# End of the first layer of a two-layer graph kernel: the last tile's scores and sums put ahead of older pairs' norms and tables, its own rows gathered first, the late diagonals made by VectorE

## What is computed

```python
h = relu(layernorm(x))
Qn = cos_normalize(h @ Wq.T);  Kn = cos_normalize(h @ Wk.T)
att = softmax(where(adj > 0, Kn @ Qn.T, NEG), axis=1)
x = x + 0.5 * (att @ h) + 0.5 * h          # first layer; a row with no edge keeps h
h = relu(layernorm(x))
g = h @ W.T + b_W
e = leaky_relu((g @ a1)[:, None] + (g @ a2)[None, :] + b_a)      # slope 0.2
x = x + softmax(where(adj > 0, e, NEG), axis=1) @ g              # second layer
```

## Time and profile before

| what | value |
|---|---|
| median of 3 runs | 1582.53 us (1582.44 to 1582.91) |
| the profiled execution | 1582.28 us, its span 1580.3 us |
| TensorE busy, share of the span | 1084.1 us, 69% |
| VectorE | 1142.5 us, 72% |
| ScalarE | 964.1 us, 61% |
| GpSimd | 1078.5 us, 68% |
| last piece of the adjacency matrix has landed | 805 us |
| first gather of the second layer | 891.49 us |

### The profile page before, as it was taken

How to read it: one execution, slowest core, us unless ns; L and a number is a source line. 1 busy time by engine, 2 the same in 40 slices (tenths; PEclk the granted TensorE clock), 3 DMA queues, 4 the chain that set the end, 5 groups by cost and what they waited for, 6 DMA issues and landing times.

```text
span 1580.3 us, 21879 instructions
## 1 busy us (share of the span) xinstructions
PE 1084.1 (69%) x5729; PEld 815.3 (52%) x5729; DVE 1142.5 (72%) x4489; ACT 964.1 (61%) x2795; POOL 1078.5 (68%) x1121
## 2 busy tenths in 40 slices
PE   6977777788867877877775456556555665555556
PEld 4653545555555555554565335445444554445445
DVE  6995698879887888888776256566666676656666
ACT  5663867778778777877678644454445444544423
POOL 2246777677776767776676377777777777777774
PEclk9997899989999988999888666787788777777777
DMA  9999999999999999999942122222222222222221
GB/s 361 421 388 390 374 399 400 403 347 400 398 394 365 399 399 377 399 398 402 395 169 53 44 55 61 61 60 61 58 61 60 61 59 60 61 60 60 59 60 41
DMA packets 90474, 358.45 MB, mean 227 GB/s; under 512 B 23653, under 2 KB 36328, under 8 KB 57576
## 3 DMA queue, kind: packets, MB, share of 16 engines
q1 hardware_dynamic: 49128, 277.05, 44.1%
q0 software_dynamic: 34304, 71.42, 17.2%
q10 hardware_dynamic: 6912, 8.52, 1.5%
HBM read 344.18 MB, written 12.72 MB: 226 GB/s over the span
## 4 chain that ended last, share of the span: by engine, by line
POOL 36%; DMA 27%; issue 14%; PE 11%; DVE 6%; ACT 5%; SPq 0%; ACTq 0%; POOLq 0%; DVEq 0%
DMA arena<-in_adj_dram 25%; POOL arena L542 19%; POOL arena L537 13%; PE ps L1029 5%; POOL arena L967 3%; DMA arena<-tab,idx_shared 2%; PE ps L1052 2%; POOL arena L975 2%; ACT prod L1217 2%; PE ps L1064 1%; PE ps L1066 1%; DVE norm L1381 1%; ACT R L1187 1%; ACT R L1185 1%; PE ps L1010 1%
## 5 line engine op out<-in xcount | busy, mean ns | idle before, releaser
L967 POOL DMA_INDIRECT arena<-tab,idx_own x320 | 322.2, 1007 | 128.5 <-issue 92.4
L542 POOL DMA_INDIRECT arena<-tab,idx_own x320 | 303.0, 947 | 97.5 <-issue 97.5
L1029 PE MATMUL ps<-arena,fold 128*128 128x512 fp8e4 x1024 | 285.8, 414 | 108.4 <-DMA arena<-in_adj_dram 108.2
L607 ACT ACTIVATE arena<-arena,negm 128x773 f32<-128x773 f32 (+1 forms) x64 | 58.5, 914 | 362.8 <-DVE negm L681 362.8
L975 POOL DMA_INDIRECT arena<-tab,idx_shared x216 | 210.5, 974 | 93.3 <-issue 57.5
L537 POOL DMA_INDIRECT arena<-tab,idx_shared x216 | 204.1, 945 | 87.4 <-issue 65.5
L557 PE MATMUL ps<-prod,column 128*128 128x384 f32 (+1 forms) x128 | 103.2, 905 | 231.2 <-DVE prod L633 231.2
L1029 PEld LDWEIGHTS ps<-arena,fold 128*128 128x128 bf16 x1024 | 91.7, 101 | 258.7 <-DMA arena<-in_adj_dram 153.5
L1217 ACT ACTIVATE prod<-prod,arena 128x128 f32<-128x128 f32 x528 | 203.4, 390 | 0.0
L633 DVE TENSOR_TENSOR prod<-ident,arena 128x384 f32<-128x384 f32 (+3 forms) x70 | 39.5, 571 | 220.7 <-DMA arena<-tab,idx_shared 220.7
L580 PEld LDWEIGHTS ps<-arena,diag 128*128 128x128 f32 x640 | 142.8, 315 | 45.6 <-issue 40.9
(11 more groups left out here) (202 smaller groups left out, 2496.7 us busy)
## 6 DMA issues: line engine op xcount, KB each, us to landing
arena<-in_adj_dram SPq DMA_DIRECT2D x256, 1024.0 KB
arena<-tab,idx_own POOLq DMA_INDIRECT x640, 2.7
arena<-tab,idx_shared POOLq DMA_INDIRECT x432, 2.6
tab<-arena ACTq DMA_DIRECT2D x16, 260.0 KB, 7.4
tab<-tw ACTq DMA_DIRECT2D x32, 130.0 KB
res<-in_x_dram SPq DMA_DIRECT2D x8, 512.0 KB, 11.8
out_dram<-arena SPq DMA_DIRECT2D x64, 64.0 KB, 1.7
prod<-in_L_gnn_Wq_dram SPq DMA_DIRECT2D x1, 64.0 KB
```

What stands on the lines that cost most here:

```text
L542: pool.indirect_dma_start(out=GO[q][:, s, :], out_offset=None, in_=tab1, in_offset=bass.IndirectOffsetOnAxis(ap=idx_own[:, t, s:s + 1], ax ...
L607: nc.scalar.activation(sc[p][:, 0:K + n * P], sc[p][:, 0:K + n * P], ACT.Exp, bias=negm[:, p:p + 1]).then_inc(s_ex1, 1)
L967: pool.indirect_dma_start(out=G[t % GR][:, s, :], out_offset=None, in_=tab0, in_offset=bass.IndirectOffsetOnAxis(ap=idx_own[:, t, s:s + 1] ...
L1029: last = nc.tensor.matmul(keys_ps[t % 2], fold[:, PIECE_BITS * f + b, :], ring8[m % RING][:, b * WORDS:(b + 1) * WORDS], start=False, stop ...
```

## The change

It touches only the end of the first layer, and one order in `scalar_rows`.

1. **Diagonals.** `diags` of tiles 58 and later leave ScalarE. VectorE makes them as one product of 640 elements a partition, identity times the spread weights, right behind `spill_weights` of the same tile; `last_diags` of tile 63 is two such products (three slots, two slots).
2. **Gathers.** GpSimd gathers tile 63's own slots before its shared chunks.
3. **ScalarE.** Tile 63's own scores come first, then its shared ones, all before the transposed copy of pair 28 and the rows of pair 28.
4. **TensorE.** The sums of tiles 62 and 63 stand directly behind those of tile 61, ahead of the projection of pair 28 and of pair 29. Within tile 63 the own part comes first.
5. **VectorE.** Tile 63's own products come ahead of the spill weights of tile 62, its shared product behind all diagonals, its spill weights ahead of `finish` of tile 61.
6. **`scalar_rows`.** For every pair the store is issued right behind `tw`, and the second column follows.

```diff
+    LATE = T - 6
...
                 nc.scalar.activation(tw[:, :, 0:D + 1], got_ps[:, :, 0:D + 1], ACT.Copy).then_inc(self.rows, 1)
+                act.wait_ge(self.rows, 2 * i + 1)
+                act.dma_start(self.rows_at(tab1, 2 * i, 2), tw[:, :, :]).then_inc(self.stored, 16)
                 nc.scalar.activation(s1_all[:, 2 * i:2 * i + 2], got_ps[:, :, D + 1], ACT.Identity,
                                      bias=c0[:, :]).then_inc(self.rows, 1)
-                act.wait_ge(self.rows, 2 * i + 2)
-                act.dma_start(self.rows_at(tab1, 2 * i, 2), tw[:, :, :]).then_inc(self.stored, 16)
...
                 pool.wait_ge(s_pv, T - GR)
-                gather_shared(T - 1)
                 gather_own(T - 1, 0, 3, s_g[0][(T - 1) % GR])
                 gather_own(T - 1, 3, K, s_last)
+                gather_shared(T - 1)
...
                 def weighted_last(t):
                     p, q, n = t % 2, t % GR, PAIRED[t % QT]
-                    pe.wait_ge(s_W, paired(t + 1))
                     pe.wait_ge(s_fin, t - 1)
-                    for j in range(n):
-                        v, s, e = shared(t, SPAN[t % QT][0] + j)
-                        nc.tensor.matmul(pv_ps[p][:, 0:ROW], W[p][j], Gc[:, e, :], start=j == 0, stop=False)
                     for part, (a, b) in enumerate(((0, 3), (3, K))):
                         pe.wait_ge(s_dg, t + 1 + part)
                         for s in range(a, b):
-                            last = nc.tensor.matmul(pv_ps[p][:, 0:ROW], diag[t % DR][:, s, :], G[q][:, s, :], start=False,
-                                                    stop=s == K - 1)
+                            nc.tensor.matmul(pv_ps[p][:, 0:ROW], diag[t % DR][:, s, :], G[q][:, s, :], start=s == 0,
+                                             stop=False)
+                    pe.wait_ge(s_W, paired(t + 1))
+                    for j in range(n):
+                        v, s, e = shared(t, SPAN[t % QT][0] + j)
+                        last = nc.tensor.matmul(pv_ps[p][:, 0:ROW], W[p][j], Gc[:, e, :], start=False, stop=j == n - 1)
                     last.then_inc(s_pv, 1)
...
                 weighted(T - 3)
+                weighted(T - 2)
+                weighted_last(T - 1)
                 second.tensor_pr(pe, PAIRS - 4)
-                weighted(T - 2)
                 second.tensor_tr(pe, PAIRS - 3)
                 second.tensor_pr(pe, PAIRS - 3)
-                weighted_last(T - 1)
...
-                    if t >= 2:
+                    if 0 <= t - 2 < LATE:
                         diags(t - 2)
...
                 second.scalar_hT(act, PAIRS - 5)
-                weights(T - 2)
+                scores(T - 2, 0, slots(T - 2))
+                exps(T - 2)
                 second.scalar_h(act, PAIRS - 4)
                 second.scalar_rows(act, PAIRS - 5)
-                last_scores(T - 1, K, slots(T - 1), 1)
-                last_exps(T - 1, K, slots(T - 1), 3, 1)
+                last_scores(T - 1, 0, 3, 1)
+                last_exps(T - 1, 0, 3, 3, 1)
+                last_scores(T - 1, 3, K, 2)
+                last_exps(T - 1, 3, K, K, 2)
                 second.scalar_root(act, PAIRS - 3)
+                last_scores(T - 1, K, slots(T - 1), 2 + len(runs(T - 1)))
+                last_exps(T - 1, K, slots(T - 1), slots(T - 1), 3)
                 second.scalar_hT(act, PAIRS - 4)
-                last_scores(T - 1, 0, 3, 2)
-                last_exps(T - 1, 0, 3, 6, 2)
-                last_diags(T - 1, 0, 3, 2)
                 second.scalar_h(act, PAIRS - 3)
                 second.scalar_rows(act, PAIRS - 4)
-                last_scores(T - 1, 3, K, 3)
-                last_exps(T - 1, 3, K, 8, 3)
-                last_diags(T - 1, 3, K, 3)
                 second.scalar_hT(act, PAIRS - 3)
...
+                def diags(t):
+                    if t >= DR:
+                        dve.wait_ge(s_pv, t - DR + 1)
+                    dve.wait_ge(s_ex, t + 1)
+                    nc.vector.tensor_tensor(diag[t % DR][:, 0:K, :], repeat(ident[:, :], K), spread(weight[t % 4][:, 0:K], P),
+                                            ALU.mult).then_inc(s_dg, 1)
...
                     if t >= 3:
                         spill_weights(t - 3)
+                        if t - 3 >= LATE:
+                            diags(t - 3)
...
+                def last_diags(t, first, end, n):
+                    dve.wait_ge(s_ex, t + n)
+                    dve.wait_ge(s_pv, t - DR + 1)
+                    nc.vector.tensor_tensor(diag[t % DR][:, first:end, :], repeat(ident[:, :], end - first),
+                                            spread(weight[t % 4][:, first:end], P), ALU.mult).then_inc(s_dg, 1)
+
                 second.vector_stats(dve, link, PAIRS - 4)
                 spill_weights(T - 3)
+                diags(T - 3)
                 finish(T - 5)
                 dve.wait_ge(s_red, red(T - 2))
+                last_own_products(T - 1, 0, 3, s_g[0][(T - 1) % GR], go_before[(T - 1) % GR])
+                last_own_products(T - 1, 3, K, s_last, 32)
+                spill_weights(T - 2)
+                diags(T - 2)
+                last_diags(T - 1, 0, 3, 1)
+                last_diags(T - 1, 3, K, 2)
                 spill_products(T - 1)
-                spill_weights(T - 2)
-                last_own_products(T - 1, 0, 3, s_g[0][(T - 1) % GR], go_before[(T - 1) % GR])
                 finish(T - 4)
                 second.vector_stats(dve, link, PAIRS - 3)
-                last_own_products(T - 1, 3, K, s_last, 32)
+                spill_weights(T - 1)
                 finish(T - 3)
-                spill_weights(T - 1)
                 finish(T - 2)
```

12 lines of the change are left out of this document (1 added, 11 removed).

## The result

| | before | changed |
|---|---|---|
| median of 20 runs each, us | 1582.69 | 1585.0 |
| lowest and highest | 1579.45, 1585.21 | 1582.21, 1588.31 |
| profiled execution, its span | 1582.28, 1580.3 | 1582.42, 1580.3 |

A forecast was written before the change was run, and what follows sets the result against it. The second layer's last table store was taken to decide the time. To the median of 1582.53, +0.45 for the string of pairs and +0.8 for held gathers gave 1583.8, rounded down to 1583.7 us; range 1580.9 to 1586.4.

The forecast's parts named there:

- What bounds: Second layer runs at GpSimd's own pace, moving as a block; the issue of its last table store, at 888.43, decides.
- Part 1: ScalarE gives away diagonals, 1.5 us a tile; tile 62's scores start 3 us earlier, but VectorE is late next.
- Part 2: VectorE takes on the diagonals, 0.8 us per product; its queue sets the last sums' start, 5.7 us earlier.
- a start near 873 to 875: Sign for Part 2: in the changed profile, tile 63's last sums on TensorE start near 873 to 875.
- VectorE has no gap of over 1 us: Sign in the changed profile: VectorE's queue shows no such gap between 855 and 872.
- Part 3: Pairs 28 to 31 queue behind the last sums through one PSUM bank; last store at 888.9, +0.45 us.
- Part 4: GpSimd's gathers held by VectorE products land 1 to 2.9 us later, 0.9 covered; +0.8 taken.
- I take +0.8: Part 4's term: delay that held gathers put on the start of the string behind the last sums, +0.8 us.
- the sum without holds: VectorE's summed queue from 855.28, letting TensorE start tile 63's sums at 873.2, with no gather held.
- 0 to 2: Part 4's range in us for what late gathers add to the string's start, after 0.9 us of cover.
- held gathers: Rival: last gathers land after 868.8, string slips 2.9 us, one more slow pair adds 0.5; 1586.4, chance 0.18.
- the gain arrives: Rival: string behind the last sums stays 9.55 us, so the store comes 5.7 us earlier; 1576.9, chance 0.05.

The follow-up runs named there:

- e3: Changed kernel with the diagonals of tiles 58 to 63 made by ScalarE again, all else as changed; ratio 1.0029 to the kernel before.
- e1: Changed kernel with TensorE's sums of tiles 62 and 63 and ScalarE's transposes of pair 28 back in the earlier order; ratio 0.9985 to the kernel before.
- e5: Kernel before with only the changed order of pairs on TensorE and ScalarE; gathers, products and diagonals as before; ratio 1.0031 to the kernel before.
- e7: Changed kernel with diagonals of tiles 58 to 61 written as five VectorE operations with one tensor operand each; ratio 1.0011 to the kernel before.
- e9: e2 with tile 63's sums split and its shared scores and sums ahead of pair 29's work, VectorE reordered; ratio 0.9988 to the kernel before.
- e2: e1 with older pairs' work on ScalarE and VectorE filling waits for tile 63's last rows; 1577.94 us, ratio 0.9965 to the kernel before.

## Why the prediction was right

The kind of result and the range came out; the figure was 1.3 us short of the median, and two of its terms were off in opposite directions (Parts 3 and 4). By its steps, in the profiled execution:

- *What bounds.* Right. The last table store decides, and the second layer moved as a block.
- *Part 1, ScalarE.* Right in kind: tile 62's weights are there 2.2 us earlier from the mark (861.63 − 820.34 = 41.3, 865.87 − 822.38 = 43.5 before; 3 were predicted, and tile 62's owners' matmuls took 1.1 us longer here), and VectorE is late next. e3 shows the part to be worth 2.3 us.
- *Part 2, VectorE's queue.* The product was priced well: 0.73 us in the queue (855.86 to 856.59) against 0.8. The queue itself came out as summed but for two waits for rows, 0.63 and 1.65 us. So the last sums start 2.6 us earlier from the mark where 5.7 were summed: 2.0 went to these waits and 1.1 to tile 62's owners' matmuls. The sign that I had named, a start near 873 to 875, came out (874.26) only because this execution was 2 us ahead as a whole; the sign that VectorE has no gap of over 1 us did not come out (1.65).
- *Part 3, the string.* Right, and the deciding step. 12.5 us from pair 28's projection to the last store, 13.2 predicted (3.65 + 4.56 + 4.56 + 0.4). The clock fell during the last two pairs, but the first of them was slow for half only: from table to table 4.14 us (880.40 to 884.54) and 4.39. e1 and e5 are the proof from both sides.
- *Part 4, the held gathers.* **The term that was mis-sized**: "I take +0.8". From the first of tile 63's five own gathers to the first shared one it was 9.06 us (854.48 to 863.54) instead of 6.25, the shared rows landed at 870.0, 1.65 us after VectorE was free, and tile 63's first sums started 19.9 us after VectorE came out of its checks (874.26 − 854.32), where the sum without holds has 17.9 (873.2 − 855.28). So +2.0, the end of the "0 to 2" that I had given. I took a value under its middle, but two holds followed each other in the one tile that had no cover. The rule of the Trainium skill, "SBUF — State Buffer", "Who interferes with whom", that the second comer blocks while a VectorE instruction with two SBUF inputs runs, agrees with the trace in the main: of the gathers that start well inside such a product nearly all are held, but the hold lasts 0.82 us beyond the product, and the two at 863.54 and 864.78 were not held. The same section's inference that such products leave descriptor generation alone does not agree, and e7's timelines decide it. One reading of mine was too strong: of the 29 gathers over 1.2 us before the change, 25 start within a product of 256 or more elements to a partition, three start 0.07 to 0.08 us ahead of one, and one (613.35, 1.26 us) starts beside two products of 128x128.
- *Not in the sum:* tile 62's owners' matmuls took 3.45 us at 844.13, at the lower clock, and 2.35 before; +1.1 in this execution. The ten experiments have 2.38 to 3.45 for the same matmuls, whose order the edits leave alone. The changed order doesn't force the slow value (2.46 in e1, 2.38 in e7, 2.39 in e9), so I take it for spread; whether it makes it more frequent isn't shown, since only two executions (2.35, and 2.81 in e5) have the order of before.

The account: +1.25 predicted, +1.2 for the holds, +1.1 for the clock at tile 62's owners, −0.7 for the string give +2.9 at the last store, where the traces differ by 2.96. The medians differ by 2.3; the 1.1 belongs to this one execution, so how much of it stands in the medians isn't known. The rival "held gathers" had the right mechanism; its 1586.4 took the slip of 2.9 and a slow pair on top, which the medians don't show. The rival "the gain arrives" fell as argued: its condition, a string of under 10 us, is what e1 and e2 make true, and there the gain does arrive.

What stays open: whether a form of diagonals that holds no gather pays (e7's ratio is within the spread), why the clock at tile 62's owners differs from run to run, why e1's last store took 4.62 us to land, and what e2 gains on e1.

## What to carry to other kernels

Work that is put ahead of older work is only early if the older work isn't a chain that ends the stage as well: add up what stands *behind* the moved step, on every engine, down to the event that releases the next stage. Leave a serial chain (here one PSUM bank between ScalarE and TensorE) running, and put the urgent work into its holes; e1 and e2 turn a loss of 0.16% into gains of 0.15% and 0.35% with the same instructions. Where the profiled executions end alike, count from a mark behind the last thing that the change can't touch.
